# Four layers on one core: where a token choice layer copies its expert outputs, how it loads the second expert weights, and in which order it combines, normalises and selects

## What is computed

```python
grouped = x.reshape(x.shape[:-2] + (-1, ne, d))                  # groups of 16 tokens
logits = jnp.einsum('...btd,des->...btes', grouped, controller)  # 64 experts
logits = logits + tie
perm = (logits == jnp.max(logits, axis=-3, keepdims=True))
sel = jnp.einsum('...btd,...btes->...besd', grouped, perm)
inner = jax.nn.relu(jnp.einsum('...besd,desf->...besf', sel, f1) + bias)
inter = jnp.einsum('...besf,esfd->...besd', inner, f2)
out = jnp.einsum('...besd,...btes->...btd', inter, perm)
```

## Time and profile before

| what | value |
|---|---|
| median of 3 runs | 2849.27 us (2844.29 to 2855.34) |
| profiled execution, its own time | 2839.36 us |
| span of that execution, first to last instruction | 2837.5 us |
| mean granted TensorE clock | 0.928 of full speed |
| TensorE busy in the span | 2315.9 us, 82% |
| VectorE busy | 1485.0 us, 52% |
| ScalarE busy | 886.6 us, 31% |
| GpSimd busy | 677.7 us, 24% |
| DMA | 329.19 MB, mean 116 GB/s |

### The profile page before, as it was taken

How to read it: one execution, slowest core, us unless ns; L and a number is a source line. 1 busy time by engine, 2 the same in 40 slices (tenths; PEclk the granted TensorE clock), 3 DMA queues, 4 the chain that set the end, 5 groups by cost and what they waited for, 6 DMA issues and landing times. The chain is left out here.

```text
span 2837.5 us, 44896 instructions
## 1 busy us (share of the span) xinstructions
PE 2315.9 (82%) x18544; PEld 1432.9 (50%) x18544; DVE 1485.0 (52%) x2615; ACT 886.6 (31%) x1257; POOL 677.7 (24%) x404
## 2 busy tenths in 40 slices
PE   2899999999999985677675598894598898889896
PEld 1455555555555455565563266553355555555553
DVE  2445555555555544455454165547556756766662
ACT  0233333333333333333341121220143333334332
POOL 4121112221111201131431433433102113202212
PEclk7899999999999997898888799997699999999997
DMA  6455664555565404675676210102443244235230
GB/s 144 93 105 111 118 123 99 114 113 104 114 117 115 98 24 148 221 257 178 212 240 208 78 60 30 60 30 66 143 129 97 78 144 144 73 103 159 84 91 16
DMA packets 227353, 329.19 MB, mean 116 GB/s; under 512 B 15072, under 2 KB 164944, under 8 KB 226896
## 3 DMA queue, kind: packets, MB, share of 16 engines
q1 hardware_dynamic: 224336, 325.68, 43.0%
q10 hardware_dynamic: 2816, 0.65, 0.1%
HBM read 197.71 MB, written 127.93 MB: 115 GB/s over the span
## 5 line engine op out<-in xcount | busy, mean ns | idle before, releaser
L1678 ACT ACTIVATE l1f_probs<-l1f_slot 128x1024 f32<-128x1024 f32 x240 | 240.6, 1022 | 423.1 <-PE l1f_slot L1851 252.3
L518 DVE TENSOR_REDUCE l0a_rowmax<-l0a_slot 128x4 f32<-128x1024 f32 (+1 forms) x256 | 293.4, 1156 | 128.4 <-PE l0a_slot L631 125.5
L461 ACT ACTIVATE l0a_probs<-l0a_slot 128x1024 f32<-128x1024 f32 (+1 forms) x256 | 248.4, 971 | 338.0 <-PE l0a_slot L621 189.0
L1741 DVE TENSOR_REDUCE l1f_rowmax<-l1f_slot 128x1 f32<-128x1024 f32 x240 | 287.6, 1219 | 100.5 <-PE l1f_slot L1837 100.3
L1851 PE MATMUL l1f_slot<-l1f_Qs,l1f_Ks 128*128 128x256 f32 x960 | 184.5, 319 | 42.9 <-DVE l1f_rowmax L1741 16.8
L1851 PEld LDWEIGHTS l1f_slot<-l1f_Qs,l1f_Ks 128*128 128x128 f32 x960 | 141.6, 200 | 113.2 <-ACT l1f_probs L1678 30.3
L1837 PE MATMUL l1f_slot<-l1f_Ks,l1f_Qs 96*128 96x512 f32 x480 | 170.7, 449 | 29.2 <-DMA l1f_Qs<-kq_rows 12.7
L421 POOL TENSOR_TENSOR l0a_turned<-l0a_turned 128x512 f32<-128x512 f32 x32 | 40.7, 1272 | 560.8 <-DVE l0a_turned L504 560.8
L621 PE MATMUL l0a_slot<-l0a_mask,l0a_ident 128*128 128x512 bf16 (+1 forms) x512 | 150.4, 376 | 25.7 <-issue 23.4
L1796 PE MATMUL l1f_os<-l1f_probs,l1f_V 128*32 128x256 f32 x1920 | 165.8, 398 | 1.8 <-ACT l1f_probs L1678 0.9
L563 PE MATMUL l0a_O<-l0a_probs,l0a_V 128*32 128x128 f32 x3840 | 156.5, 279 | 10.6 <-issue 10.6
(11 more groups left out here) (190 smaller groups left out, 4069.3 us busy)
## 6 DMA issues: line engine op xcount, KB each, us to landing
expert_outputs<-l0f_inter SPq DMA_DIRECT2D x64, 512.0 KB, 3.7
l0f_wide<-expert_outputs SPq DMA_DIRECT2D x32, 1024.0 KB, 10.2
l0a_Qs<-qk_rows SPq DMA_DIRECT2D x96, 256.0 KB, 7.8
l0a_Ks<-qk_rows SPq DMA_DIRECT2D x96, 256.0 KB, 14.8
l1f_Ks<-kq_rows SPq DMA_DIRECT2D x48, 512.0 KB, 6.7
qk_rows<-l0a_hi SPq DMA_DIRECT2D x32, 512.0 KB, 2.8
qk_rows<-l0a_lo SPq DMA_DIRECT2D x32, 512.0 KB, 4.2
l0f_f<-in_dram SPq DMA_DIRECT2D x32, 512.0 KB, 5.1
```

What stands on the lines that cost most here:

```text
L461: exp_ready.by(act.activation(probs[:, t % 2, HG * g:HG * g + HG, 0:reach, :], s[:, :, 0:reach, :], ACT.Exp, scale=SCALE))
L518: max_ready.by(dve.reduce_max(rowmax[:, t, :, 2 * g:2 * g + 2], s[:, :, :, first:2 * P], AX))
L1678: exp_done.by(act.activation(probs[:, half, u - FIRST[i], :], s[:, :], ACT.Exp, scale=SCALE))
L1741: max_done.by(dve.reduce_max(rowmax[:, 2 * u + t:2 * u + t + 1], s[:, :], AX))
```

## The change

Only the token choice layer is edited.

- The buffers `inter` and their wait go. ScalarE and VectorE copy expert outputs into `wide`, which the combination of the half before has finished reading, and SyncE stores from there. `spare` and `best`, which lay in `wide`, become places of their own (`choice` has two halves).
- `f2` has room for one half (16 pairs, 2 MB); one transfer loads it, a step "f2": in the first half right behind the gather of X-1, in the second behind store and load of x.
- The last selections of a half alternate with combinations; in the second half transposes of X+1 stand ahead of the third combination, the logits ahead of the fourth.
- The marking of the second half ("second") moves between the expert steps, as do hi and lo; spreading the first half moves from VectorE to ScalarE.
- The aggregate moves from behind the last combination to behind the second h step of the next block. Of the 16 tiles GpSimd normalises eight, VectorE the other eight during the next selection.
- The first transposes wait for the identity alone; the other constants are waited for ahead of the logits.

```diff
-    steps = [(-1, "gather", 1)] + selection(0)
-    steps += combination(-1, 1) + [(0, "spread", 1)]
-    steps += merged(experts(0), [(-1, "rescale", n) for n in range(4)])
-    steps += [(0, "gather", 0)] + merged(selection(1), [(-1, "store", n) for n in range(2)] + [(1, "load", n) for n in range(2)])
-    steps += combination(0, 0) + [(1, "hi", 0), (1, "lo", 0), (1, "hi", 1), (1, "lo", 1)]
-    steps += [(1, "xT", n) for n in range(2 * CH)] + [(1, "logits", 0)]
-    steps += experts(1)
+    s, e, late = selection(0), experts(0), combination(-1, 1)
+    steps = [(-1, "gather", 1), (0, "f2", 0)] + s[:10] + merged(s[10:], late) + [(0, "spread", 1)]
+    steps += e[:4] + [(-1, "aggregate", 0)] + e[4:] + [(0, "gather", 0)]
+    s, e, early = selection(1), experts(1), combination(0, 0)
+    steps += merged(s[:10], [(-1, "rescale", n) for n in range(4)] + [(-1, "store", 0), (-1, "store", 1), (1, "load", 0), (1, "load", 1), (0, "f2", 1)])
+    steps += merged(s[10:], early[:2]) + [(1, "xT", 0), (1, "xT", 1), early[2], (1, "xT", 2), (1, "xT", 3), (1, "logits", 0), early[3]]
+    steps += [(1, "spread", 0)] + e[:4] + [(1, "second", 0)] + e[4:6] + [(1, "hi", 0), (1, "lo", 0)] + e[6:8] + [(1, "hi", 1), (1, "lo", 1)] + e[8:]
...
-        f2 = sb("f2", [P, NR * QP, D])
+        f2 = sb("f2", [P, PAIRS, D])
...
-        inter = sb("inter", [P, NI, 4, D])
-        choice = sb("choice", [P, NQ, G])
+        choice = sb("choice", [P, 2, NQ, G])
+        best = sb("best", [P, 2, NQ])
...
+        def rescale(eng, X, n, tiles):
+            wait_alone(eng, ln.rstd_ready, ln.count(X, 0))
+            for t in tiles:
+                normed[n].by(eng.tensor_scalar(x[:, X % 2, t, :], x[:, X % 2, t, :], ln.mv[:, t, 0:1], ln.rstd[:, t:t + 1],
+                                               ALU.subtract, ALU.mult))
...
-                    left[i % NI].by(sp.dma_start(scratch[half, :, 4 * n:4 * n + 4, :], inter[:, i % NI, :, :]))
-                    k = (2 * i + 2) // QP + NR - 1
-                    if i % 2 and X + k // NK < NB:
-                        load_f2(X + k // NK, k % NK)
+                    left[half].by(sp.dma_start(scratch[half, :, 4 * n:4 * n + 4, :], wide[:, 4 * n:4 * n + 4, :]))
+                if kind == "f2":
+                    schedule.wait_filled(sp, X if i else X - 1, ("inter", IN - 1 if i else 2 * IN - 1))
+                    alone(sp)
+                    f2_loaded.by(sp.dma_start(f2[:, :, :], f2_rows[:, PAIRS * i:PAIRS * i + PAIRS, :]))
                 if kind == "gather":
-                    for l in left:
-                        l.wait(sp, X, IN // NI * (i + 1))
-                        alone(sp)
...
+                    wait_alone(sp, left[i].sem, (X + 3) * IN * 16)
...
-                if kind == "rescale":
-                    if i == 0:
...
-                    ln.normalise(pool, x[:, X % 2, :, :], x[:, X % 2, :, :], X, 0, range(4 * i, 4 * i + 4))
+                if kind == "aggregate":
...
+                    ln.reciprocal_root(pool, X, 0)
+                    rescale(pool, X, 0, range(NT))
...
+                if (kind, i) == ("spread", 0):
+                    choice_ready.wait(act, X, 1)
+                    alone(act)
+                    schedule.wait_filled(act, X - 1, ("out", NC - 1))
...
+                    for j in range(J):
+                        rows = slice(EH * j, EH * j + EH)
+                        spread_ready[0].by(act.copy(spread[rows, 0, :, j, :], choice[rows, 0, :, :]))
...
-                    inter_free(act, X, i)
-                    inter_even.by(act.copy(inter[:, i % NI, 0::2, :], s[:, 0:512].rearrange("p (e d) -> p e d", e=2)))
+                    e = 4 * (i % IN)
+                    inter_even.by(act.copy(wide[:, e:e + 4:2, :], s[:, 0:512].rearrange("p (e d) -> p e d", e=2)))
...
+                    mark(X, 0)
+                if kind == "second":
+                    mark(X, 1)
+                if kind == "aggregate":
+                    ln.aggregate(dve, X, 0)
+                if kind == "rescale":
+                    rescale(dve, X, 1, range(NT + 2 * i, NT + 2 * i + 2))
...
-                        if t == NC - 1:
-                            ln.aggregate(dve, X, 0)
```

## The result

| what | before | changed |
|---|---|---|
| median, 6 runs each on one chip | 2842.76 us (2838.96 to 2855.34) | 2827.9 us (2826.05 to 2830.89) |
| ratio, 95% interval | | 0.9941 [0.992, 0.9961] |
| profiled execution (span) | 2839.36 (2837.5) us | 2827.45 (2825.5) us |
| token choice layer in the profile | 500.8 us | 478.5 us |
| last layer in the profile | 862.5 us | 873.0 us |

The change is faster by 0.6%, 14.9 us between the medians, and the forecast of 2829 us lies 1 us beside the median. That closeness is partly luck. The forecast took 20.0 us off 2849.27, the median of the first three runs; all six runs of the kernel before have 2842.76. And as the stages show, the edited layer gave more than forecast, and the last layer, whose code the change leaves alone, took some of it away in this profile.

What follows compares the result with a forecast made beforehand. The DRAM round trip, not an engine, was taken as the bound. Terms +1.7 - 2.6 - 3.1 - 5.8 - 2.7 - 1.0 - 6.5 = -20.0 from 2849.27 gave 2829 us, range 2811 to 2845.

Steps and rivals of the forecast that it cites:

- The bound: Token choice layer: no engine bounds it, but the DRAM round trip of stores, gather, transposes and logits.
- T: Time from H to the gather's issue: 14.3 us forecast, 14.7 where hi parts are made, bounds 12.9 to 15.3.
- Weights as one load: Second expert weights, 2 MB per half queued behind the gather or store and load of x: forecast hidden in both halves.
- the rival of a shared load: The 2 MB flow alongside gather and load of x, each ending 6.4 us later: 2868 us, slower; chance 0.07.
- The last second half: Last block's second half, without a load of x: 42.45 us forecast against 45.2, a gain of 2.7.
- H: Start of the group of 48 matmuls on the second expert weights ending each half of a block; eight times.
- Combination among selections, first halves: Last selection's copy stands behind the last gathered piece, 3.5 us; halves 46.35 against 47.4, -3.1 us for three.
- Second halves with a load: Two halves loading the next x: input arrives, then 15.0 us to the experts; 65.2 against 68.1 us, -5.8 together.
- Normalisation split: Uncovered layer end: GpSimd and VectorE take 8 tiles each, second store costs 3.1 more; -6.5 us.
- lock rival: VectorE and GpSimd take turns normalising, 12.9 instead of 9.7 us in the uncovered end: 2832 us; chance 0.10.
- unmoved gather: Rival: something other than weights limits the stores, T stays 17.6, 18.2, 17.5; 2853 us, no measurable change; chance 0.13.
- full rate: Rival: T is 12.9 everywhere and the remaining 512 KB weight load counts too; -42 us, 2808 us; chance 0.10.

Runs made afterwards that it cites:

- the version with all three edits: Changed kernel with first-half selection before combinations, last block's weights ahead of stores of x, VectorE's aggregate and marking behind the copies: 2800.28 us, ratio 0.9845.
- the edit alone: Changed kernel with the first half's selection finished before its four combinations, as before the change: 2814.29 us, ratio 0.9904 to the kernel before.

## Why the prediction was right, and where not

*The bound.* Right. It is the round trip through DRAM; with weights back among the stores all of the gain was gone, and with waiting copies three quarters.

*T.* Forecast 14.3 (14.7 in halves that make the hi parts), measured 14.4 in X = 0 and 14.0 in the halves with hi, but 15.7 to 15.8 in the other first halves; the mean of all eight is 14.5. Three parts make these numbers up. Where nothing stands in front of the copies and the stores end cleanly T is 12.6, below the lower bound of 12.9: the stores alone flow faster than the 330 GB/s of the earlier trace rows. VectorE's work in front of the copies, the aggregate or the second marking, each some 1.4 us in three halves, adds 1.2 to 1.6, as the experiment shows; ScalarE's casts cost nothing (12.7 with them). And in the halves of 14.4 and 15.7 the stores have a tail, which adds some 1.7 us. That the forecast lies near the mean is luck: it took the stores slower than they are, and left out the aggregate and the tail. These are three stretches of 1 us before the gather at 1247.32 in the changed kernel, the tail in the last two:

```profile
1241.00:1242.00 1.00, 1.00 (x11) 1.00 (x10) 0.98 (x4) 0.91 (x3) 1.00 (x2) 1.00 1.04 410
...
1245.00:1246.00 1.00, 1.00 (x11) 1.00 (x10) 0.66 (x1) 0.66 (x2) 1.00 (x2) 1.00 0.07 25
1246.00:1247.00 1.00, 0.69 (x6) 0.45 (x5) 0.52 (x2) 0.95 (x3) 1.00 (x2) 1.00 0.05 20
```

*Weights as one load.* Right in the first halves: the gather's last piece is used 15.7 us after the gather's issue (1200.19, 1215.90), no later than with nothing behind it (16.1 and 16.0 in the other two first halves, 16.1 and 16.2 before), and the second halves with a load aren't longer either. So the 2 MB behind the gather take nothing from it, and the rival of a shared load falls.

*The last second half* is **the step that failed**: forecast 42.45, measured 50.5. "In the other half it is queued behind store and load of x and ends near 50 after H, needed near 60" holds where a load of x, transposes and logits stand in between. The last block has none of these: the same queue place, and the weights are needed some 20 us sooner, about 40 after H. By the terms of the forecast: T was 15.8 for 14.3, the last combination started 18.7 us after the gather's issue for 16.1, and from there to H it was 16.0 for 12.05. The last of these is the late weights: loading them ahead of the stores gave 4.1 back. The middle one is TensorE's clock in the main: the first combination took 3.68 instead of 1.95 us at 1.2 GHz, behind 6.05 us of idling. In the version with all three edits the terms were 14.5, 16.2 and 11.8, and the half took 42.5, the forecast value. The waits for VectorE's sums ahead of the last two combinations (0.27 and 1.41 us) were the same there (0.28 and 1.41), so they aren't what made the half long.

*Combination among selections, first halves.* The mechanism was right, with the copy behind sum and statistics (3.5 forecast, 3.6 measured from 1217.85, the combination's end, to 1221.47) and 46.35 forecast for 45.5, as T was 14.0 and not 14.7 in front of them. The experiment shows the price of the new order: 3.8 us from the last combination to the experts, of which the edit alone gave back some 2 us per half, and the last version all of it in two halves, where the clock stayed full.

*Second halves with a load.* 65.2 forecast, 63.5 measured, though T in front of them was 1.5 longer than taken. The term mis-sized is the arrival of x: the transposes start 23.5 and 23.3 us after the gather's issue, not 25.8. SyncE issues the load of x 17.5 us after the gather, against 20.2 in the half from which the 25.8 was read (18.7 in the other one). The "15.0" from there to the experts was 14.2 and 14.4, with both combinations in it at their full 1.95 us. The experiment shows only that leaving them out would gain 0.8 and not 3.9. In the second half of X = 0 (58.6 forecast, 56.2 measured) it is the same two terms: 17.9 us for 19.2, and 13.9 for 15.0.

*Normalisation split.* -6.5 forecast, -6.2 in the two profiles, 6.3 by the experiment. The lock rival falls: VectorE's tiles took 0.43 us each beside GpSimd's 1.24. The Trainium skill (SBUF — State Buffer, practical consequences) has one of the two blocked for the whole of the other's instruction if VectorE is in a two-port mode, which no row here tells; at tiles of this size the trace shows no blocking, while beside GpSimd's long memset VectorE was held up.

*Sum.* The failed step (8.0 us too little) and the overpriced ones (2.4, 2.5 and 3.5 us in three lines of the table, 1.7 in the final T) nearly cancelled: -20.0 and -22.3. Of the other rivals, the unmoved gather is out by T, and full rate was half true: T reaches 12.6 where VectorE is free and no tail follows, but in the first halves the slower clock took back what that gave, until the last version.

## What to carry to other kernels

When a transfer is moved within a queue, work out its deadline for each instance of the loop, the last one above all, where the work that gave it time is missing. Price an inserted step by the gaps it fills and by what stands behind it, not by its duration: leaving out two combinations of 1.95 us would have gained 0.8 where they filled waits, while a copy that the next stage needed, put behind another's sum, cost 3.8 us. An edit that brings nothing alone may only have moved the wait: in the last half VectorE's work late brought 0.5 us, since the wait for the weights grew to 5.79, the weights ahead brought 4.1, and all three edits together 8.0. And before an earlier arrival is called worthless, look at the granted clock of the group behind it: here 1.1 us gained and 1.7 lost to the clock looked like no effect.

## What the runs showed that was not expected

- Stores of expert outputs with nothing between them flow at 393 to 418 GB/s in stretches of 1 us of the half shown, against a mean of 330 with weight loads among them.
- Behind some groups of stores DMA still moves 20 to 25 GB/s for 2 us, as in the two last rows above, and the gather has to wait for it. In that stretch there is one transfer of the instruction queue (transfers, MB, share of the engines' time):

```profile
q8 instruction: 1, 0.02, 0.8%
```

  Over the 64 halves of eight profiles (the changed kernel twice, and the six versions without loads or waits put back) the tail goes with the time of that transfer. In all 38 halves where it lay within 9 us of the gather's issue the tail was there (20 GB/s or less in the last us); in the 23 where it lay more than 10 us ahead of it, or where there was none, it wasn't, and T was 12.6 to 14.1 us. The three halves in between had all or part of it. The same half of one kernel falls on either side (14.0 and 15.7 us in the second half of X = 0 in the two profiles). Whether the transfer causes the tail was not tried.
- The last layer, the same code in all twelve profiles, took 862.5 to 876.5 us, with granted clocks of 0.91 to 0.94 in the second part of the three shown: a scatter as large as most effects here.
